# The fourth attention's score bias: from VectorE's addition to two TensorE matmuls with a unit matrix

## The reference, cut to what matters

```python
x = x + _L3_attn_ref(_layernorm(x, axis=-1), ..., L3_attn_rel_bias)

def _L3_attn_ref(x, Wq, bq, Wk, bk, Wv, bv, Wo, bo, gamma, beta, rel_bias):
    xn = (x - mu) * rsqrt(var + 1e-05) * gamma + beta
    q = (xn @ Wq.T + bq).reshape(Bx, Nx, H, D).transpose(0, 2, 1, 3)   # k and v likewise
    attn = einsum('bhnd,bhmd->bhnm', q, k) * scale
    M = _interp_matrix(Nx, 32)
    rel = einsum('ni,hij,mj->hnm', M, rel_bias, M)      # last row and column set to 0
    attn = attn + rel[None]
    attn = where(triu(ones, k=1), -inf, attn)           # causal mask
    attn = softmax(attn, axis=-1)
    out = einsum('bhnm,bhmd->bhnd', attn, v) ...
    return out @ Wo.T + bo
```

## Time and profile before

| | |
|---|---|
| median of 3 runs | 2553.05 us (2552.40 to 2559.71) |
| the profiled execution: its time | 2557.27 us |
| its span, first to last instruction | 2555.3 us |
| TensorE busy | 1864.2 us, 73% of the span |
| VectorE busy | 1314.5 us, 51% |
| ScalarE busy | 1093.2 us, 43% |
| GpSimd busy | 745.8 us, 29% |
| mean granted TensorE clock | 0.82 of full speed |

### The profile page before, as it was taken

The page is one execution under the profiler, slowest core; times in us unless marked ns, Lnnn a source line. Parts: engine busy times, 40 slices in busy tenths (PEclk is TensorE's granted clock), DMA queues, the critical chain, the costliest instruction groups (busy, mean ns, idle before and its releaser), DMA issues. The chain is left out here.

```text
span 2555.3 us, 39295 instructions
## 1 busy us (share of the span) xinstructions
PE 1864.2 (73%) x14689; PEld 1299.7 (51%) x14689; DVE 1314.5 (51%) x3517; ACT 1093.2 (43%) x2105; POOL 745.8 (29%) x625
## 2 busy tenths in 40 slices
PE   3876305897764897978999485997788868862895
PEld 1544203334453465766798353665545535552674
DVE  3887595201122675454343363775278847761223
ACT  3664402332221675843344243773346536630331
POOL 1232101272225321116455001321212122227353
PEclk9888756899655898877999586998879869965897
DMA  4111320024442500001476200000000000001224
GB/s 147 82 82 83 87 79 4 1 82 116 126 108 67 202 2 19 17 13 50 130 235 198 68 1 13 14 10 9 3 1 2 1 13 14 10 23 57 67 79 135
DMA packets 140655, 156.38 MB, mean 61 GB/s; under 512 B 19889, under 2 KB 126065, under 8 KB 139537
## 3 DMA queue, kind: packets, MB, share of 16 engines
q1 hardware_dynamic: 126644, 122.79, 15.5%
q0 software_dynamic: 13248, 28.21, 3.3%
q10 hardware_dynamic: 576, 2.88, 0.3%
HBM read 120.54 MB, written 68.57 MB: 74 GB/s over the span
## 5 line engine op out<-in xcount | busy, mean ns | idle before, releaser
L2696 POOL DMA_INDIRECT f_back<-f_ys,f_row x158 | 151.2, 957 | 177.8 <-DVE f_ys L2857 148.6
L836 PE MATMUL a_AV<-a_vx,a_pT 128*64 128x18 f32 (+1 forms) x3072 | 115.1, 223 | 48.9 <-DVE a_att L529 31.6
L836 PEld LDWEIGHTS a_AV<-a_vx,a_pT 128*64 128x64 f32 x3072 | 105.8, 146 | 79.3 <-issue 32.3
L2689 POOL DMA_INDIRECT f_slots<-f_pay,f_slot x128 | 124.2, 971 | 66.0 <-issue 38.2
L536 DVE TENSOR_REDUCE a_mx<-a_S 128x16 f32<-128x1024 f32 x96 | 117.5, 1224 | 41.0 <-PE a_S L812 39.0
L823 PE MATMUL a_TP<-ident,a_e 128*128 128x128 f32 x768 | 112.6, 295 | 32.7 <-ACT a_e L689 32.2
L823 PEld LDWEIGHTS a_TP<-ident,a_e 128*128 128x128 f32 x768 | 95.9, 152 | 65.6 <-ACT a_e L689 55.4
L689 ACT ACTIVATE a_e<-a_e 128x1024 f32<-128x1024 f32 x96 | 101.3, 1055 | 65.4 <-DVE a_e L539 65.4
L694 ACT COPY a_pT<-a_TP 128x512 f32<-128x512 f32 x192 | 104.1, 589 | 58.2 <-PE a_TP L823 58.0
L812 PE MATMUL a_S<-a_kbd,a_qT 64*64 64x512 f32 x768 | 118.0, 691 | 0.1
L539 DVE TENSOR_TENSOR a_e<-a_S,a_mx 128x1024 f32<-128x1024 f32 x96 | 117.1, 1219 | 1.9
(11 more groups left out here) (478 smaller groups left out, 4724.4 us busy)
## 6 DMA issues: line engine op xcount, KB each, us to landing
f_wt<-in_f_ew SPq DMA_DIRECT2D x39, 584.0 KB
f_slots<-in_blank SPq DMA_DIRECT2D x1, 18576.0 KB
f_wt<-in_f_leaf SPq DMA_DIRECT2D x94, 98.0 KB, 2.0
f_pay<-f_back SPq DMA_DIRECT2D x8, 1024.0 KB, 8.2
f_xs<-f_slots SPq DMA_DIRECT2D x47, 144.0 KB
f_slots<-in_blank SPq DMA_DIRECT2D x1, 5760.0 KB
f_xs<-leaf_slots SPq DMA_DIRECT2D x22, 256.0 KB, 3.0
leaf_out<-f_ys SPq DMA_DIRECT2D x22, 256.0 KB, 2.2
```

What stands on the lines that cost most here:

```text
L836: last = pe.matmul(AV[64 * c:64 * c + 64, 2 * hp * W1:2 * (hp + 1) * W1], pT[:, hp, 64 * c:64 * c + 64], vx[:, g % 2, t, c, 2 * hp:2 * hp ...
L2689: pool.indirect_dma_start(out=slots[:, :], out_offset=bass.IndirectOffsetOnAxis(ap=slot[:, c, t:t + 1], axis=0), in_=pay[:, c, t, :], in_o ...
L2696: pool.indirect_dma_start(out=back[:, :], out_offset=bass.IndirectOffsetOnAxis(ap=row[:, i % RR, t:t + 1], axis=0), in_=ys[:, i % RY, t, : ...
```

## The change

VectorE's addition in PSUM is dropped. In its place TensorE, right behind the four score matmuls of a unit, adds the table with two matmuls into the same banks: stationary is the unit matrix (128 x 128), moving are the 512 columns of each half of `bt`, with `start=False` so that PSUM accumulates. The semaphore `scores` is raised by the last of these. It holds for `a3` alone; the other attentions have no bias.

```diff
             def highest(i):
                 v.wait_ge(scores.sem, scores.after(i))
-                if bias:
-                    links.link(v, v.tensor_tensor(unit(i), unit(i), bt[:, :, :], ALU.add))
                 return v.tensor_reduce(mx[:, i % 2, :], unit(i), AX.X, ALU.max)
...
                         last = pe.matmul(S[64 * c:64 * c + 64, i % 2, r, :], qT[rows, g % 2, SL * b:SL * b + SL],
-                                         kbd[rows, g % 2, b, :, :], start=True, stop=True)
+                                         kbd[rows, g % 2, b, :, :], start=True, stop=not bias)
+                if bias:
+                    for r in range(2):
+                        last = pe.matmul(S[:, i % 2, r, :], k.ident[:, :], bt[:, 8 * r:8 * r + 8, :], start=False, stop=True)
                 last.then_inc(scores.sem, 1)
```

## The result

The changed kernel takes 2566.32 us in the median of 20 runs (2555.13 to 2580.25), the kernel before 2552.91 in 20 (2546.12 to 2560.33). The ratio is 1.0055, 95% interval 1.0042 to 1.0067: slower by 0.55%, 13.4 us between the medians. The profiled execution of after took 2565.62 us with a span of 2563.4, against 2557.27 and 2555.3.

The account below looks back on a forecast made before the run. Bound by a ring between TensorE and VectorE, with TensorE's clock down to 0.87. Steps +8.0, opening +0.4, end +0.6 make +9.0 us: 2566.3 on the profiled execution, 2562.1 on the median, forecast 2563, range 2555 to 2576.

Parts of the forecast that it names:

- The frame: Fourth attention: its new time is built from the second attention's, plus a pair of TensorE matmuls in each unit.
- 50.75 - 5.9: Fourth attention's 29 steps: 1.75 us per pair added, less 5.9 us of waits that go in five t=1 steps.
- The opening: Fourth attention, first score group to that of unit 2: 10.2 us against 9.8, +0.4 us.
- The end: Fourth attention, last score group to start of the last update: 14.85 us against 14.26, +0.6 us.
- The steps: Fourth attention, score group of unit 2 to that of unit 31: 178.0 us against 170.01, +8.0 us.
- The clock: TensorE in the fourth attention: granted clock 1.00 from unit 2 to unit 31, where it averaged 0.87.
- Rival 2: Fourth attention's clock still falls, averaging 0.87: steps 204.6 us, sum +36 us, 2589 us; chance 0.09.
- The pair's price: TensorE, fourth attention: 1.75 us per pair of matmuls, between bounds of 1.72 and 2.04 us.
- Rival 3: Changing between quarter and whole matmul shape costs every turn: pair 2.04 us, sum +18 us, 2571 us; chance 0.07.
- rival 4: The pair's matmuls overlap on TensorE: pair 0.86 us, sum -18.6 us, 2534 us, so faster; chance 0.04.
- Rival 1: The pair hides in TensorE's idle time in the fourth attention: sum +3.9 us, 2557 us, not slower; chance 0.20.
- the +9.0: Whole kernel: sum of 8.0 for steps, 0.4 for opening and 0.6 us for end.

Follow-up runs that it names:

- e1: Kernel after with the pair deleted and VectorE's addition not put back, so no bias or mask: ratio 0.987 to before, 29 steps in 134.2 us.
- e4: Kernel after with the table split into two bfloat16 parts, four one-pass matmuls in place of the pair: ratio 0.9930 to before.
- e7: Kernel after with the pair of unit i+2 moved ahead of weigh(i), opening the accumulation that the scores add to: ratio 0.9999 to before.
- e9: Kernel before run again unchanged for one more trace: 2553.48 us, 29 steps in 166.4 us.
- e10: Kernel before run again unchanged for a third trace: 2560.67 us, 29 steps in 173.6 us.

## Why the prediction was right, and where it was not

- **The frame** (the stage is `a1` plus a pair) held to 1.0 us: e1 gives 134.2 where `a1` has 133.2, and the pair adds 45.0 us to it, where the prediction's terms are 50.75 - 5.9 = 44.85. The opening came to 10.26 for 10.2. The end came to 14.84 for 14.85, but by luck: in e1 it is 12.84 where `a1` has 13.10, and the pair adds 2.0 us to it, not 1.75.
- **The steps**: forecast 178.0, measured 179.19. At t=3 and t=0 the pair adds 1.71 (6.74 for 5.03, 6.14 for 4.43), at t=1 0.59 (6.25 for 5.66, forecast 0.57). The step t=2 is 5.94 us where `a1` has 3.99, but e1 has 4.18: 0.19 of it is gamma and beta, and the pair adds 1.76. The term mis-sized is thus the 133.17 us taken over from `a1`: without the bias this stage takes 134.19, which is 1.0 of the 1.2 us. In the last units, without other products, the step is 5.63 us for 3.75. There weigh waits for `take_values`, as predicted: it ends 0.06 us ahead of weigh in after and in e1. The profile of after names ScalarE's copy as the releaser, but weigh starts 1.11 us behind the start of the copies here and only 0.72 at t=2, where it does wait for them. The shift is 1.88 us and not 1.75, because the maximum starts 3.11 us behind the score group where it started 1.23 behind it in e1.
- **The clock**: 1.00 from unit 2 to unit 31, as forecast. Rival 2 is out, in two traces.
- **The pair's price**: 1.82 to 1.83 us from its start, 1.71 in a step. The product behind it is shorter by 0.12 us at t=3, from its start to the next (0.85 us, 0.97 in e1): it no longer stands right behind the quarter matmuls. Rival 3 (2.04) and rival 4 (overlap, and the 0.52 us per matmul estimated from two pages) are out. A bfloat16 matmul in e4 takes 0.22 us, a quarter of the 0.86. The four of them, 0.88 us, lie under the 1.46 us that the prediction gave as the price for a gain, and e4 is a gain.
- **Rival 1** was half right: the waits could be filled, but only by another order (e7), which comes to the time of before. Its 173.9 us for the steps should read 172.9 (178.0 - 4.2 - 0.9); its sum of +3.9 is right.
- **What I read wrongly in before**: I put all 18 us between 151.9 and 170.0 down to the lower clock. Two of the 29 steps hold a stall of VectorE of 3.4 us each, 6.7 us in all; I took the earlier trace rows as a fall of the clock and did not ask why TensorE had been idle ahead of it. The same stalls stand in VectorE's 145 us: it was to fall to 109 and fell to 102.9. The number came out right since after loses neither: its L453 ran 1 us ahead of L386 in every group.
- **Luck in the base**: the +9.0 is counted from the one profiled execution of before, whose stage took 194.1 us. In e9 it took 190.4 and in e10 198.3, from which the same forecast of 203.1 would have been +12.7 and +4.8. The profiled one lies at the mean of the three.
- **The total**: the stage is slower by 10.2 us in the profiled pair, and by 9.2 in the steps and about 1 in opening and end over the three and two traces. The medians differ by 13.4, with an interval of 10.7 to 17.1 us. Some 3 us are not placed. The rest of the kernel, whose instructions are the same, takes 2360.5 to 2361.2 us in the three traces of before and 2359.1 and 2366.9 in the two of after, so it scatters by more than that; whether its median moved is open. My sum of +9 to +10 was 3 to 4 us short.

## What to carry to other kernels

An addition moved from VectorE to TensorE is paid at TensorE's rate: 512 float32 columns cost 0.86 us here, so a pair costs 1.7 us against 1.23 for the addition. In this stage TensorE, without the pair, was idle for only 11 us of 134 (e1), and so nearly all of the price showed. Two bfloat16 parts of a constant table cost half of that. A table that can open the accumulation belongs where TensorE waits anyway, not between the scores and their reader. And when TensorE's clock is low, look first at what TensorE waited for just before: in two places here it was a tiny instruction behind a long GpSimd one, and that had to be told apart from the ordinary waits, which remained.

## What the hardware showed that I had not expected

- A VectorE instruction with 128 x 4 numbers in SBUF took 3.51 us when it started 0.12 us behind a GpSimd multiplication of 3.60 us, and 0.15 us otherwise. They met in 2, 2 and 4 of 5 groups in three executions of the same program, whose 29 steps took 166 to 174 us; it is one part of that scatter, beside the clock.
- With the work moved to TensorE the stage became even: 179.19 and 179.20 us in two executions, at full clock. The executions as a whole still differed by 7.7 us.
